# Softmax weights turned by VectorE and through DRAM, and a new order around them in the attention loop of a decoder layer

## What is computed

```python
q, k, v, s, g = x @ Wq, x @ Wk, x @ Wv, clip(x @ Ws, -32, 32), x @ Wg     # 64, 64, 128, 64, 128 columns a head
z = cumlogsumexp(s, axis=time); p = exp(s - z)
# key states: hk decays by the slot, adds k_t (x) p_t;   ok_t = q_t . hk_t      (64 slots)
pv = softmax(ok)                                          # the "weights"
# value states: hv decays by the slot, adds p_t (x) v_t; o_t = pv_t . hv_t      (128)
o = o * rsqrt(mean(o * o) + eps) * g_norm * silu(g)
x = layernorm(x + concat_heads(o) @ Wo)
```

## Time and profile before

| | us |
|---|---|
| median of three runs | 1826.91 (1825.39 to 1828.23) |
| the profiled execution | 1825.38 |
| its span, first to last instruction | 1823.7 |
| pair loop, steps 2 to 28, in it | 841.36 |
| TensorE / VectorE / ScalarE / GpSimd busy | 1781.5 / 1421.3 / 754.8 / 594.2 |

### The profile page before, as it was taken

How to read it: one execution, slowest core, us unless ns; L and a number is a source line. 1 busy time by engine, 2 the same in 40 slices (tenths; PEclk the granted TensorE clock), 3 DMA queues, 4 the chain that set the end, 5 groups by cost and what they waited for, 6 DMA issues and landing times.

```text
span 1823.7 us, 39286 instructions
## 1 busy us (share of the span) xinstructions
PE 1781.5 (98%) x15604; PEld 1303.6 (71%) x15604; DVE 1421.3 (78%) x2555; ACT 754.8 (41%) x1885; POOL 594.2 (33%) x595
## 2 busy tenths in 40 slices
PE   9999999999999999999998799999999999999998
PEld 7788888888887888888886644443434488888886
DVE  5778887878888788888787889999999665555556
ACT  3433333333333333333333248888888622122223
POOL 3042250443332513514432332344423233232332
PEclk9999999999999999999999889999999999999999
DMA  4425334442434252434333001111111111111102
GB/s 149 125 64 145 82 97 113 104 123 77 117 101 126 62 150 77 111 100 120 85 89 96 3 20 29 28 28 29 29 29 20 25 22 29 20 28 25 21 15 92
DMA packets 218550, 127.91 MB, mean 70 GB/s; under 512 B 100096, under 2 KB 198144, under 8 KB 218368
## 3 DMA queue, kind: packets, MB, share of 16 engines
q1 hardware_dynamic: 218368, 125.40, 27.0%
HBM read 72.90 MB, written 44.30 MB: 64 GB/s over the span
## 4 chain that ended last, share of the span: by engine, by line
PE 87%; DVE 5%; ACT 3%; SPq 2%; DMA 2%; issue 1%; POOL 0%; POOLq 0%; DVEq 0%; ACTq 0%
PE a_ps L61 20%; PE a_ps L62 19%; PE a_ps L63 19%; PE a_ps L1137 6%; PE a_ps L1099 5%; PE a_ps L1121 3%; PE a_ps L1081 2%; ACT x_prob L1809 2%; PE a_ps L1332 2%; PE a_ps L1153 2%; PE a_ps L1321 1%; PE a_ps L1267 1%; PE a_ps L1253 1%; PE a_ps L1144 1%; PE a_ps L1295 1%
## 5 line engine op out<-in xcount | busy, mean ns | idle before, releaser
L1873 DVE TENSOR_REDUCE a_raw_qks<-a_ps 128x1 f32<-128x512 f32 x512 | 321.2, 683 | 19.8 <-PE a_ps L1099 19.0
L1809 ACT ACTIVATE x_prob<-a_ps 128x512 f32<-128x512 f32 x512 | 280.0, 609 | 63.4 <-PE a_ps L1121 61.8
L61 PE MATMUL a_ps<-a_vg_hi,a_xT_lo 128*128 128x512 f32 x512 | 207.0, 404 | 0.3 <-DVE a_eT L1910 0.3
L63 PE MATMUL a_ps<-a_vg_hi,a_xT_hi 128*128 128x512 f32 x512 | 200.6, 392 | 0.0
L62 PE MATMUL a_ps<-a_vg_lo,a_xT_hi 128*128 128x512 f32 x512 | 200.1, 391 | 0.0
L917 POOL TENSOR_TENSOR a_f<-a_rs 128x8 f32<-128x8 f32 x32 | 6.4, 199 | 584.6 <-ACT a_flat L1719 584.6
L61 PE MATMUL a_ps<-a_xT_hi,a_qks_lo 128*128 128x512 f32 x384 | 157.2, 409 | 0.4 <-DVE a_xT_lo L1904 0.4
L62 PE MATMUL a_ps<-a_xT_lo,a_qks_hi 128*128 128x512 f32 x384 | 150.7, 392 | 0.0
L63 PE MATMUL a_ps<-a_xT_hi,a_qks_hi 128*128 128x512 f32 x384 | 149.6, 390 | 0.0
L1099 PE MATMUL a_ps<-a_xT_lo,a_xT_hi 64*128 64x512 f32 x384 | 143.8, 462 | 5.1 <-DMA a_xT_lo<-a_xT_lo 2.5
L1719 ACT ACTIVATE a_flat<-a_ps 128x128 bf16<-128x128 f32 x256 | 67.3, 278 | 181.8 <-PE a_ps L1332 174.4
(11 more groups left out here) (205 smaller groups left out, 4107.3 us busy)
## 6 DMA issues: line engine op xcount, KB each, us to landing
a_og_blocks<-a_og_turn SPq DMA_DIRECT2D x120, 128.0 KB, 2.4
a_og_turn<-a_og_blocks SPq DMA_DIRECT2D x30, 512.0 KB, 4.4
a_e_blocks<-a_e_turn SPq DMA_DIRECT2D x124, 64.0 KB, 1.8
a_e_turn<-a_e_blocks SPq DMA_DIRECT2D x31, 256.0 KB, 3.2
a_z_blocks<-a_og SPq DMA_DIRECT2D x124, 64.0 KB, 2.5
a_key_blocks<-a_causal SPq DMA_DIRECT2D x124, 64.0 KB, 3.4
a_causal<-a_key_blocks SPq DMA_DIRECT2D x31, 256.0 KB, 2.8
a_raw_vg<-in_L_attn_Wv_dram SPq DMA_DIRECT2D x8, 512.0 KB, 5.6
```

What stands on the lines that cost most here:

```text
L61: pe.matmul(out, w_lo, x_hi, start=start, stop=False)
L63: return pe.matmul(out, w_hi, x_hi, start=False, stop=stop)
L1809: nc.scalar.activation(prob[par][:, s % 4, :], score_bank(q, s, par), ACT.Exp, scale=X_SCALE).then_inc(exp_done[par], 1)
L1873: nc.vector.tensor_reduce(nm[:, q % 2, i % 4, par, i // 4:i // 4 + 1], max_bank(u, q, i, par), AX.X, ALU.max, negate=True).then_inc(max_re ...
```

## The change

In steps 0 to 28 (`n <= LATE_OUT`) four things differ. Steps 29 to 31 keep the old form.

1. TensorE's four transposes of the weights and ScalarE's copy out of the bank are gone. VectorE transposes 32x32 blocks of `pv` into `weights_turn` (the half of `flat` that held the scan) right behind the scaled weights (`turn_weight_rows`). SP writes them to DRAM behind the gets of z and in front of the get of the keys, and reads them back behind the latter. ScalarE copies them into `wT`, which is now the half that held `pv` (`rows_of_weights`), behind its copy of the key rows, which itself moves behind Q's copy.
2. On TensorE, Q and the output projection of the step before follow VG+3 at once; diagonal blocks and values from states come behind them.
3. Key scores of step n+1 are written between the values from states and the values of step n. They wait for the mask of step n's diagonals (`diag_masked`), which reads the same banks. The values wait for `values_begun` in place of `proj_done`, both counts of TensorE's own.
4. On VectorE the mask of the diagonals moves from between the reciprocals of z to behind the third add; the fourth add follows it.

Several semaphores are merged into one (`first_turned`, `qks_hi_ready`, `wo_scaled`) with the same order of waits.

```diff
+        weights_turn = flat[:, 0:T].rearrange("p (s i x) -> p s i x", s=4, x=32)
+        wT = flat[:, T:2 * T]
...
+            def put_weights(n):
+                sp.wait_ge(weights_turned, n + 1)
+                wait(sp, weights_back, 16 * n)
+                put_blocks(weight_blocks, weights_turn, weights_out)
+            def get_weights(n):
+                sp.wait_ge(weights_out, 64 * (n + 1))
+                get_blocks(weight_blocks, weights_turn, weights_back)
...
                 get_z(n + 1)
+                if n <= LATE_OUT:
+                    put_weights(n)
                 get_keys(n + 1)
+                if n <= LATE_OUT:
+                    get_weights(n)
...
-                key_scores(n)
+                if first or n > LATE_OUT + 1:
+                    key_scores(n)
...
-                transpose_weights(n)
+                if n > LATE_OUT:
+                    transpose_weights(n)
...
+                if n <= LATE_OUT:
+                    next_project(Q)
+                    if not first:
+                        project_out(n, pair0, (0, 1, 2, 3))
+                pe.wait_ge(wT_ready, n + 1)
                 diagonals(n)
                 values_from_states(n)
...
-                next_project(Q)
-                if not first and n <= LATE_OUT:
-                    project_out(n, pair0, (0, 1, 2, 3))
...
-                pe.wait_ge(proj_done, PROJ * (n + 2))
+                if n <= LATE_OUT:
+                    key_scores(n + 1)
+                    pe.wait_ge(values_begun, n + 1)
...
                 values(n, j)
...
-                rows_of_keys(n + 1)
+                if n > LATE_OUT:
+                    rows_of_keys(n + 1)
                 next_proj(VG + 3)
                 next_proj(Q)
+                if n <= LATE_OUT:
+                    rows_of_keys(n + 1)
+                    rows_of_weights(n)
...
                 scaled_weights(n)
+                if late:
+                    turn_weight_rows(n)
...
                     inverse_z(n + 1, (0,))
-                    mask_diagonal_blocks(n)
                 gating(n + 1, VG + 3, b1)
...
                 inverse_z(n + 1, (1,) if late else (0, 1))
                 if not first and late:
-                    add_out(n, (j - 1) % B, (0, 1, 2, 3))
+                    add_out(n, (j - 1) % B, (0, 1, 2))
+                if late:
+                    mask_diagonal_blocks(n)
+                if not first and late:
+                    add_out(n, (j - 1) % B, (3,))
                 gated_output(n, j, 0)
```

More of the change, by code:

```diff
@@ L267, in layer_program @@
         o_done = sem("o_done")
-        e_done = sem("e_done")
+        first_turned = sem("first_turned")
         queries_kept = sem("queries_kept")
@@ L285, in layer_program @@
         z_back = sem("z_back")
-        zT_done = sem("zT_done")
+        values_begun = sem("values_begun")
         weights_ready = sem("weights_ready")
+        weights_turned = sem("weights_turned")
+        weights_out = sem("weights_out")
+        weights_back = sem("weights_back")
         eT_ready = sem("eT_ready")
@@ L888, in split_s @@
                 pool.wait_ge(raw_s_in, (p + 1) * 16)
-                split(raw_qks[:, :, 0, :], qks_hi[:, :, 0, :], qks_lo[:, :, 0, :], s_hi_ready, s_ready, p + 1)
+                split(raw_qks[:, :, 0, :], qks_hi[:, :, 0, :], qks_lo[:, :, 0, :], qks_hi_ready, s_ready,
+                      3 * p + (2 if p else 1))
             def split_k(p):
                 pool.wait_ge(raw_qk_in, (p + 1) * 32)
-                split(raw_qks[:, :, 2, :], qks_hi[:, :, 2, :], qks_lo[:, :, 2, :], k_hi_ready, k_ready, p + 1)
+                split(raw_qks[:, :, 2, :], qks_hi[:, :, 2, :], qks_lo[:, :, 2, :], qks_hi_ready, k_ready,
+                      3 * p + (1 if p else 2))
             def split_q(p):
                 pool.wait_ge(raw_qk_in, (p + 1) * 32)
-                split(raw_qks[:, :, 1, :], qks_hi[:, :, 1, :], qks_lo[:, :, 1, :], q_hi_ready, q_ready, p + 1)
+                split(raw_qks[:, :, 1, :], qks_hi[:, :, 1, :], qks_lo[:, :, 1, :], qks_hi_ready, q_ready, 3 * p + 3)
             def split_vg(p):
@@ L1320, in values_from_states @@
                     for h in range(2):
-                        pe.matmul(ob[h][HALF[r ^ h], i * P:(i + 1) * P],
+                        mm = pe.matmul(ob[h][HALF[r ^ h], i * P:(i + 1) * P],
                                   wT[HALF[h], (c ^ h) * CHUNK:((c ^ h) + 1) * CHUNK],
                                   state[HALF[h], c - 1, :], start=(c == 1 or c == 2), stop=False, skip_group_check=True)
+                if n <= LATE_OUT:
+                    mm.then_inc(values_begun, 1)
             def values(n, j):
@@ L1338, in transpose_e @@
                 pe.wait_ge(eT_ready, m + 1)
-                transpose4(tb, [eT[:, m % 2, i * P:(i + 1) * P] for i in range(TT)]).then_inc(e_done, 1)
+                transpose4(tb, [eT[:, m % 2, i * P:(i + 1) * P] for i in range(TT)]).then_inc(first_turned, 1)
             def transpose_keys(m):
@@ L1343, in transpose_keys @@
                 wait(pe, wT_ready, m)
-                transpose4(okb, [keys[:, i * P:(i + 1) * P] for i in range(TT)]).then_inc(keysT_done, 1)
+                transpose4(okb, [keys[:, i * P:(i + 1) * P] for i in range(TT)]).then_inc(first_turned, 1)
             def transpose_z():
                 pe.wait_ge(scan_done, 1)
-                transpose4(ob[0], [running[:, i * P:(i + 1) * P] for i in range(TT)]).then_inc(zT_done, 1)
+                transpose4(ob[0], [running[:, i * P:(i + 1) * P] for i in range(TT)]).then_inc(first_turned, 1)
             def transpose_weights(n):
@@ L1410, in step @@
                     max_pair(0, 3)
-                next_project(Q)
-                if not first and n <= LATE_OUT:
-                    project_out(n, pair0, (0, 1, 2, 3))
+                if n > LATE_OUT:
+                    next_project(Q)
                 if into:
                     max_pair(0, 4)
-                pe.wait_ge(proj_done, PROJ * (n + 2))
+                if n <= LATE_OUT:
+                    key_scores(n + 1)
+                    pe.wait_ge(values_begun, n + 1)
+                else:
+                    pe.wait_ge(proj_done, PROJ * (n + 2))
                 values(n, j)
@@ L1700, in turned_weights, with rows_of_weights @@
             def turned_weights(n):
-                act.wait_ge(pvT_done, n + 1)
-                if n < NSTEP - 1:
-                    wait(act, z_turned, n + 1)
+                act.wait_ge(pvT_done, n - LATE_OUT)
                 nc.scalar.copy(wT, tb).then_inc(wT_ready, 1)
+            def rows_of_weights(n):
+                act.wait_ge(weights_back, 16 * (n + 1))
+                nc.scalar.copy(wT.rearrange("p (i b r) -> p b i r", i=TT, b=4), weights_turn).then_inc(wT_ready, 1)
             def copy_e(m):
-                act.wait_ge(e_done, m + 1)
+                act.wait_ge(first_turned, 1)
                 nc.scalar.copy(e[:, :, :].rearrange("p i c -> p (i c)"), tb).then_inc(e_ready, 1)
@@ L1753, in step @@
                 next_proj(VG + 2)
-                turned_weights(n)
+                if n > LATE_OUT:
+                    turned_weights(n)
                 if at(n, 1):
@@ L2056, in scaled_weights, with turn_weight_rows @@
                     .then_inc(weights_ready, 1)
+            def turn_weight_rows(n):
+                dve.wait_ge(weights_ready, n + 1)
+                dve.wait_ge(z_turned, n + 1)
+                nc.vector.transpose(weights_turn, pv.rearrange("p g m -> p (g m)").rearrange("p (i s r) -> p s i r", i=TT, s=4))\
+                    .then_inc(weights_turned, 1)
             def slot_reciprocals(n):
```

17 lines of the change are left out of this document (6 added, 11 removed).

## The result

The changed kernel takes 1843.35 us (median of four, 1839.09 to 1844.34) against 1826.41 for the kernel before (1825.39 to 1828.23): a ratio of 1.0082, 95% interval 1.0068 to 1.0096. It is slower, as forecast, and 8 us above the time that the forecast named (1835.4). The profiled execution is its quickest, 1839.09 with a span of 1837.4, so between the two profiles there are 13.7 us.

What follows compares the result with a forecast made beforehand. VectorE's chain was taken to bound the changed loop: step 31.47 against 31.16, +8.4 us over 27 steps, +0.14 in step 0, total +8.5, giving 1833.9, or 1835.4 as median; own range 1829 to 1846.

Steps and rivals of the forecast that it cites:

- TensorE's saving, 0.82 us a step: TensorE's order: 0.45 from dropped weight transposes and 0.37 from diagonal and state blocks no longer standing alone.
- The wait for the mask, 0.26: Next key scores on TensorE wait for VectorE's mask of the diagonals in the same banks; 0.26 us stays open each step.
- a gain of up to 0.1 us: First values matmul: a wait on TensorE's own count is met earlier, up to 0.1 us a step less, -3 us.
- VectorE's chain: From first gated output to third output tile: sets the pace, mean 25.29 us, step 31.47 against 31.16; chance 0.56.
- X: Start of VectorE's first gated output (L2076) in a step, from which the chain's times are counted.
- The wait in nearly each step: Third output tile: TensorE waits 0.6 to 0.9 us for VectorE's first add in nearly each step.
- a wait for a gating only takes from the one at the third tile: Q's projection behind the turn: a wait under 0.8 us only shortens that for the first add.
- The turn at nothing: VectorE's 0.70 us turn of the weights before the subtraction: free under 1.18 us idle; uncovered, 20 us.
- The round trip hidden and its traffic free: Weights through DRAM ready at 626.5, diagonals due 627.3: nothing charged; rival of late weights 1865 us, chance 0.07.
- The clock: Steps 2 to 28: full granted clock expected; rival of clock loss at 0.8 us waits, 1930 us, chance 0.03.
- Steps 0, 1 and the end: Step 0 costed at +0.14 us, step 1 even, steps 29 to 31 keeping the old form.
- The states' part: Step 0: x transposes wait for VectorE's states, and these for the turn of the weights, 0.70 us.

Runs made afterwards that it cites:

- experiments 4: Against the changed kernel: key scores put back behind the values, and the reciprocal's second half behind the first two adds; 1815.83 us, ratio 0.9937.
- experiment 6: The order alone, plus key scores behind the values and the reciprocal's second half behind the first two adds; 1822.98 us, ratio 0.9977.
- Experiment 7: Mask in two halves, on top of the edits of experiments 4: by head 1828.76 us, 1.0006; by columns, with the start of experiment 8, 1813.81 us, 0.9923.
- experiment 2: Against the changed kernel: only the second half of the reciprocal moved behind the first two adds; 1825.61 us, ratio 0.9989.
- Experiment 3: Against the changed kernel: the next key scores put back behind the values; 1830.04 us, ratio 1.0009.
- the order alone: Against the changed kernel: TensorE transposes the weights again, with no VectorE turn and no weights through DRAM; 1838.59 us, ratio 1.0060.
- experiment 8: On experiments 4: weights turned behind x's low halves in steps 0 and 1, copied before queries in step 0; 1815.27 us, 0.9925 (with mask by head, 1826.75 us).
- experiment 9: Stops seen in the column run of experiment 7; then, against that run, three 512 KB loads issued earlier in steps j = 3: 1831.93 us, ratio 1.0031.
- experiment 5: Two runs against the changed kernel: the order alone, 1838.59 us, 1.0060; turn kept but the weights' DRAM transfers left out, 1841.15 us, 1.0072.
- experiment 1: Against the changed kernel: both halves of VectorE's reciprocal moved behind the first add; 1913.53 us, ratio 1.0468.
- Column run of experiment 7: Experiments 4 with the start of experiment 8 and the mask split in two halves by columns; 1813.81 us, ratio 0.9923.
- the mask by head: Experiments 4 with the mask split in two halves by head, values one head after the other; 1828.76 us, ratio 1.0006.
- last run of experiment 9: Against the column run of experiment 7: three 512 KB loads issued ahead of the keys' and weights' gets in steps j = 3; 1831.93 us, ratio 1.0031.

## Why the prediction was right, point by point

**TensorE's saving, 0.82 us a step: right.** The sum put a step without a wait for the add at 30.60; the quick one takes 30.58. The transposes alone were 0.45 in the sum and 0.48 between experiments 4 and 6.

**The wait for the mask, 0.26: somewhat small, and the reading half right.** From the first state product to the key scores are 1.15 us in the rows above, 0.34 more than the 0.81 of work in the sum: the key scores start 0.14 after the mask's end (509.54 and 0.76, to 510.44) and not 0.06. Experiment 7 shows that TensorE's own count holds the values just as long once the mask is early. The prediction had named that count only as a gain of up to 0.1 us beside the sum, a size that no run shows; it is a second wait of the same length.

**VectorE's chain: right.** X to the subtraction (L2050) was taken as 19.54 and 0.22 for slower gets, 19.76; the mean of the 27 steps is 19.65 (20.14 in the slow step shown). X to the third tile, forecast 25.29, is 25.26 on the mean, and the third tile to the next X 6.22 against 6.18. The step, forecast 31.47, is 31.48. That the agreement is this close is partly luck, as errors of up to 0.1 us with opposite signs meet in it; that the bound is VectorE's is shown by experiment 2.

**The wait in nearly each step: the sum right, the form not.** It isn't 0.6 to 0.9 us at one place in nearly each step, but a mean of 0.6 of idle weight loads at the add, from nothing to 1.5, and 0.5 at the gatings. The prediction had said that a wait for a gating only takes from the one at the third tile. Experiment 3 shows that from the other side: with 9.5 us of gating waits gone, the wait for the add shrinks by only 2.3. It had put the gatings' waits down to the turn. For most of them that is wrong: the kernel with the order alone has no turn and 10.2 us of them, and moving the key scores back takes 9.5 away, so these are the key scores' 0.47. The other 4 us are the turn's (1.5 and 2.6 in experiment 3; none in experiment 6, which has no turn), all in the steps with j = 1.

**The turn at nothing: right while VectorE's chain is the bound.** VectorE waited 34.0 us for ScalarE's cast of the output in steps 2 to 28 before and waits 13.9 now, 0.51 a step, as forecast; the order alone has 37.1. Where TensorE is the bound it costs 0.5 us in each step with j = 1 (experiment 6).

**The round trip hidden and its traffic free: right in steps 2 to 28.** No diagonals wait for the weights there, and leaving the transfers out changes nothing (852.00 against 850.02). In experiment 8 one step has a wait of 0.7 us for them, and experiment 9 shows how thin the cover is.

**The clock: right.** 1.00 over steps 2 to 28.

**Steps 0, 1 and the end: mis-sized, and most of what the forecast missed.** Step 0 was costed at +0.14 and is +1.37; step 1 at nothing and is +0.97. The states' part was right (its x transposes wait 4.8 us for 4.1):

```profile
PE a_ps L1171 <- DVE a_state L2018: 4.8, 1, 4.8
...
PE a_ps L1271 <- ACT a_flat L1735: 1.7, 1, 1.7
PE a_ps L1171 <- DVE a_xT_lo L1940: 1.5, 1, 1.5
```

What failed is that ScalarE's queue was never walked: the copy of the weights was priced "under 1 us" and its place behind Q overlooked, harmless where the output projection follows and 1.7 us where it doesn't. Without any DMA of the weights these 1.7 us stay (experiment 5), so it is the queue; with the copy moved ahead and the turn moved back, a late get takes its place (experiment 8). In step 1 the turn stands ahead of the low halves of x (1.5 us). Steps 29 and 30 were costed at nothing and are +2.35; in the other runs this stretch reads from 95.2 to 100.2, at clocks of 0.95 to 0.90, in kernels whose code is the same there, so that I put it down to no edit. The rest, 3 us, is that the profiled execution lies 4.3 us under its median and not 1.5.

## What to carry to other kernels

When an engine's order is made shorter, list the banks and tiles that its next work reuses and who must free them: the gain stops at the first of these that another engine frees late, here one add behind 1.75 us of a reciprocal that nobody needed yet. In an engine's queue put what frees something ahead of what only has to be ready later, and price each piece before it is moved (experiment 1 made the changed kernel 3.8% slower by one wrong duration, experiment 2 made it 1.0% faster with the same idea). And walk every queue that an edit appends to in the first steps too, where the neighbour that hides it is missing, and in the steps that carry extra work: six of 27 gave nothing back here (experiment 6).

## What the runs showed of the hardware

**VectorE is slower beside GpSimd.** In the steps with j = 1 GpSimd splits new weights; two operations of VectorE with both inputs in SBUF take 0.93 and 1.27 us instead of 0.69, while the one that reads PSUM keeps its 0.65. Column run of experiment 7, VectorE in such a step, then the next step:

```profile
202.67 0.65 DVE L2072 TENSOR_TENSOR a_flat<-a_ps,a_rz 128x512 f32<-128x512 f32 x1
...
204.08 0.93 DVE L2083 TENSOR_TENSOR a_flat<-a_flat,a_mx 128x512 f32<-128x512 f32 x1
...
206.56 1.27 DVE L2093 TENSOR_TENSOR a_flat<-a_flat,a_rz 128x512 f32<-128x512 f32 x1
```

```profile
235.09 0.69 DVE L2083 TENSOR_TENSOR a_flat<-a_flat,a_mx 128x512 f32<-128x512 f32 x1
...
237.34 0.69 DVE L2093 TENSOR_TENSOR a_flat<-a_flat,a_rz 128x512 f32<-128x512 f32 x1
```

```profile
202.56 1.89 POOL L899 TENSOR_TENSOR a_wo_hi<-a_raw_qks,a_zero 128x1024 fp32r<-128x1024 f32 x1
204.53 2.74 POOL L901 TENSOR_TENSOR a_wo_lo<-a_raw_qks,a_wo_hi 128x1024 fp32r<-128x1024 f32 x1
```

These steps take 31.01 instead of 30.50 (193.04 to 224.05, against 224.05 to 254.55). It takes the turn as well: the kernel before slows by the same 0.24 and 0.57 us in these steps and loses nothing, and without the turn they are as long as the others (experiment 6). The Trainium skill (SBUF — State Buffer, SBUF: two separate sides) describes the slowing: an operation of VectorE with two SBUF inputs and one of GpSimd that reads SBUF lock each other out, and the one that comes second waits for the end of the first. The rows agree to within 0.15 us, and GpSimd's spans are rough. When the two operations of VectorE start, 0.37 us of L899 and 0.71 us of L901 are left (204.08 to 204.45, 206.56 to 207.27), and they take 0.24 and 0.58 us more than usual; both end 0.55 us after GpSimd's instruction. It is so in all six steps.

**TensorE can run out of instructions.** The stop of 0.98 us in experiment 9 ends at 530.81. From 528.2 to 531.2 the DMA record of that run has 14 packets, one of them on instruction queue 8 (16 KB; another queue of this kind has one too):

```profile
DMA packets 14, 0.03 MB, mean 10 GB/s; under 512 B 6, under 2 KB 12, under 8 KB 12
...
q8 instruction: 1, 0.02, 2.3%
```

In steps 2 to 28 the waits of TensorE list 0.5 to 2.4 us of such stops in six of the kernels that send the weights through DRAM (1.1 in the changed one) and none in the kernel before or in the three that don't send them (experiments 5 and 6); but experiment 1 and the mask by head send them too and have none, so it is a matter of timing. The packets of queue 8 say more than the counts. In the trace this one runs from 528.26 to 529.38, ends before the stop begins (529.83), and TensorE goes on 1.4 us after its end. All 15 stops of more than 0.15 us in these kernels end 1.2 to 1.6 us after the end of such a packet. And by and large the later the packet starts, the longer the stop: when it starts 0.5 us ahead of the key states the stop is 1.47 us (experiment 2), at 1.3 ahead 0.98 (the run shown), at 1.9 ahead 0.17 (the changed kernel), and at 2.0 ahead or more the run shown has none over 0.15. That this packet carries TensorE's next instructions, and that the loads hold it up, is inferred from this, not measured by itself.

**The clock falls at long waits.** With waits of 1.9 us in nearly each step the granted clock is 0.96 over steps 2 to 28, and some matmuls behind a wait start 0.43 apart, nearly twice the 0.23 (experiment 1); with waits of up to 1.1 us it stays at 1.00. Six waits of up to 3.7 us leave 0.99 (last run of experiment 9).
